# Per-head stationary blocks, K and Q turned and spread apart, and new orders on five engines

## The reference

```python
x = x + conv_block(group_norm(x))      # mask from centres of mass, relu, 3x3 conv, bias
x = x + ttt_block(group_norm(x))       # "test-time training" layer over the 784 tokens
```

```python
def step(carry, inp):                  # once per chunk, in order
    W1c, b1c = carry
    xq, xk, xv, et = inp
    Z1 = xk @ W1c + b1c
    grad = _ln_l2_bwd(Z1, xv - xk, g, bb)
    Attn1 = jnp.tril(xq @ xk.swapaxes(-1, -2))
    b1_bar = b1c - jnp.tril(et) @ grad
    Z1_bar = xq @ W1c - et * Attn1 @ grad + b1_bar
    last_eta = et[..., -1, :, None]
    W1n = W1c - (last_eta * xk).swapaxes(-1, -2) @ grad
    b1n = b1c - (last_eta * grad).sum(-2, keepdims=True)
    return ((W1n, b1n), xq + _ln(Z1_bar, g, bb, EPS_IN))
```

## Time and profile before

| | |
|---|---|
| median of 3 runs | 2133.62 us (2129.63 to 2134.75) |
| the profiled execution | 2131.73 us, its span 2129.9 us |
| PE busy, weight loads busy | 85%, 67% of the span |
| DVE, POOL, ACT busy | 73%, 63%, 55% |
| mean granted clock of TensorE | 0.632 of full speed |
| first and last start of a spread of K and Q | 474.1 and 2060.8 us |

### The profile page before, as it was taken

How to read it: one execution, slowest core, us unless ns; L and a number is a source line. 1 busy time by engine, 2 the same in 40 slices (tenths; PEclk the granted TensorE clock), 3 DMA queues, 4 the chain that set the end, 5 groups by cost and what they waited for, 6 DMA issues and landing times.

```text
span 2129.9 us, 81338 instructions
## 1 busy us (share of the span) xinstructions
PE 1804.8 (85%) x33518; PEld 1429.6 (67%) x33518; DVE 1553.4 (73%) x3818; ACT 1166.9 (55%) x2554; POOL 1336.7 (63%) x1479
## 2 busy tenths in 40 slices
PE   2868898715898988989989899998998989989887
PEld 1434454304777877778778787777777877778775
DVE  6989988416777777777777777777777777777764
ACT  2324545435556565566665556656566566565653
POOL 1253444474767776677766777667776777676763
PEclk9988999855556565555555555556555555555655
DMA  5085899843454545545455454464554545545444
GB/s 222 1 44 48 102 78 77 77 143 45 57 70 57 76 65 62 72 57 75 65 61 75 57 74 66 59 77 57 72 68 58 76 62 67 70 56 77 60 57 51
DMA packets 1148753, 148.76 MB, mean 70 GB/s; under 512 B 1128416, under 2 KB 1141984, under 8 KB 1148384
## 3 DMA queue, kind: packets, MB, share of 16 engines
q1 hardware_dynamic: 1148384, 143.57, 53.6%
HBM read 40.71 MB, written 38.54 MB: 37 GB/s over the span
## 4 chain that ended last, share of the span: by engine, by line
PE 59%; DVE 11%; ACT 8%; issue 6%; SPq 6%; DMA 6%; POOL 3%; ACTq 0%; POOLq 0%; DVEq 0%
PE p_kt L1604 11%; PE p_m L1617 8%; PE p_x L1632 7%; ACT work L820 7%; PE p_y L1674 6%; PE p_y L1632 6%; PE p_x L1656 5%; SPq L494 4%; PE p_j L1571 3%; PE p_j L1572 3%; DMA late<-work 3%; PE p_j L1573 2%; DMA xs_scratch<-work 2%; PE p_x L1623 2%; SPq L415 2%
## 5 line engine op out<-in xcount | busy, mean ns | idle before, releaser
L1604 PE MATMUL p_kt<-fold,kqk 128*128 128x16 f16 x6272 | 237.0, 180 | 143.9 <-ACT work L820 139.5
L1604 PEld LDWEIGHTS p_kt<-fold,kqk 128*128 128x128 f16 x6272 | 224.5, 117 | 183.1 <-issue 177.9
L820 ACT ACTIVATE work<-p_kt 128x256 f16<-128x256 f32 x392 | 256.6, 785 | 127.2 <-PE p_kt L1604 126.7
L1286 DVE TENSOR_TENSOR work<-work 128x256 f16<-128x256 f32 x196 | 147.8, 857 | 58.0 <-ACT work L801 58.0
L1632 PEld LDWEIGHTS p_x<-w,late 128*128 128x128 f16 x4704 | 178.1, 118 | 11.8
L1632 PEld LDWEIGHTS p_y<-w,late 128*128 128x128 f16 x4704 | 177.6, 118 | 11.1
L1656 PEld LDWEIGHTS p_x<-work,kqk 128*128 128x128 f16 x4704 | 172.2, 118 | 17.6 <-issue 13.2
L596 POOL TENSOR_TENSOR w<-wst,w 128x256 f16<-128x256 f32 x98 | 71.9, 734 | 175.2 <-ACT w L849 175.2
L1617 PE MATMUL p_m<-work,late 128*128 128x16 f16 x4704 | 164.4, 181 | 18.7 <-DVE lgt L1265 10.0
L1507 PE MATMUL p_j<-work 128*128 128x392 f16 x864 | 160.0, 347 | 22.4 <-DVE work L1101 20.7
L1617 PEld LDWEIGHTS p_m<-work,late 128*128 128x128 f16 x4704 | 160.8, 118 | 21.0 <-issue 10.8
(11 more groups left out here) (171 smaller groups left out, 4638.7 us busy)
## 6 DMA issues: line engine op xcount, KB each, us to landing
kqk<-work SPq DMA_DIRECT2D x392, 64.0 KB, 3.3
late<-work SPq DMA_DIRECT2D x392, 64.0 KB, 3.2
late<-work SPq DMA_DIRECT2D x392, 32.0 KB, 2.2
out_y<-work SPq DMA_DIRECT2D x49, 256.0 KB, 6.1
x_scratch<-late SPq DMA_DIRECT2D x24, 392.0 KB, 11.8
xs_scratch<-work SPq DMA_DIRECT2D x24, 392.0 KB, 6.3
work<-x_scratch SPq DMA_DIRECT2D x49, 192.0 KB, 3.2
work<-xs_scratch SPq DMA_DIRECT2D x48, 192.0 KB, 3.2
```

The lines of the kernel that those rows point to most:

```text
L820: last = act.activation(kqt16[:, o, g, :, :, :, :].rearrange("p q t e a -> p q (e a) t"), p_kt[:, o * SC:(o + 1) * SC].rearrange("p (q f t ...
L1286: last = dve.tensor_tensor(paired(hl16[:, c % 2, at, g:g + GP, :, :, :, 1]), in_pairs(qk[:, o, :]), paired(hl16[:, c % 2, at, g:g + GP, :, ...
L1604: mm = pe.matmul(p_kt[:, at:at + CS], part, fold16[:, :], start=True, stop=True)
```

## The change

Each head gets a block of its own in all three tiles, so that the columns of a stationary matrix step by 2 elements, 4 bytes, instead of 8. The run of bytes that a spread can copy at once becomes half as long (64 instead of 128 bytes), and there are twice as many. `fold_kq` becomes `fold_k` and `fold_q`: each turns K or Q of both groups of a half, still 32 matmuls and 512 columns of `p_kt`, and each is copied by one ACT instruction of 512 elements (`kt_copy`, `qt_copy`) in place of two of 256. The spread of the turned tile becomes two of 8 transfers each, `kt_spread` and `qt_spread`, both on SP. `z_state` and `k_dot_q` wait for the first, `outputs` for the second. `o_square` gets a tile `sqo` of its own in place of the one shared with `z_square`. Many steps get explicit waits for the reader before them. All five `turn(k)` have a new order.

```diff
-        mbd = second.cut([NG, NP, GB, CS, 2, 2], F16)
-        ktqt1 = second.cut([2, NG, NP, GB, CS, 2, 2], F16)
+        mbd = second.cut([NG, NH, GB, CS, 2], F16)
+        ktqt1 = second.cut([2, NG, NH, GB, CS, 2], F16)
...
-        kq_sets = [kqk[:, 0:2 * third].rearrange("p (s b e) -> p s b e", b=GB, e=4 * HD),
+        kq_sets = [kqk[:, 0:2 * third].rearrange("p (s b e) -> p s b e", b=GB, e=2 * HD),
...
+            def turned_spread(c, o, landed_sem):
+                part = kqt16[:, o, :, :, :, :].rearrange("p g h t a -> p (g h) (t a)")
+                whole = ktqt[c % 2][:, o, :, :, :, :, :].rearrange("p g h b t a -> p (g h) b (t a)")
+                for b in range(GB):
+                    at = slice(b * CS, (b + 1) * CS)
+                    sp.dma_start(whole[at, :, b, :], part[at]).then_inc(landed_sem, 16)
+
             @guard_chunk
             def kt_spread(c):
-                sp.wait_ge(kt_copy_done.sem, kt_copy_done.count("group1", 2 * c + 1))
+                sp.wait_ge(kt_copy_done.sem, kt_copy_done.count(2 * c + 1))
...
+                    sp.wait_ge(z_done.sem, z_done.count(2 * c - 3))
+                    sp.wait_ge(k_dot_q_done.sem, k_dot_q_done.count(c - 2))
+                turned_spread(c, 1, kt_landed.sem(c))
+
+            @guard_chunk
+            def qt_spread(c):
+                sp.wait_ge(qt_copy_done.sem, qt_copy_done.count(2 * c + 1))
...
+                turned_spread(c, 0, qt_landed.sem(c))
...
             def turn(k):
+                y_store(k - 6)
                 xs_next(k)
-                xr_load(k - 5)
-                kq_spread(k - 2)
-                y_store(k - 6)
                 m_spread(k - 3)
+                xr_load(k - 4)
                 kt_spread(k - 2)
+                qt_spread(k - 2)
+                kq_spread(k - 1)
...
+            def turned_copy(s, o):
+                g = GP * (s % 2)
+                return act.activation(kqt16[:, o, g:g + GP, :, :, :].rearrange("p g h t a -> p g a (h t)"),
+                                      p_kt[:, :].rearrange("p (g a n) -> p g a n", g=GP, a=2), ACT.Copy)
...
-                act.activation(paired(mc16[:, :, :, :, :, 0]), in_pairs(p_m[:, :]), ACT.Copy).then_inc(m_high_done.sem, 1)
+                act.activation(mc16[:, :, 0], p_m[:, :], ACT.Copy).then_inc(m_high_done.sem, 1)
...
             def kq_turned(c, o, g, h, a):
-                return ktqt[c % 2][:, o, g, h // 2, :, :, h % 2, a].rearrange("p b t -> p (b t)")
+                return ktqt[c % 2][:, o, g, h, :, :, a].rearrange("p b t -> p (b t)")
...
+            def fold(s, part_of):
+                c, g = s // 2, GP * (s % 2)
                 pe.wait_ge(kq_landed.sem(c), kq_landed.count(c))
...
+                for k in range(GP):
+                    for a in range(2):
+                        for h in range(NH):
+                            at = ((k * 2 + a) * NH + h) * CS
+                            mm = pe.matmul(p_kt[:, at:at + CS], part_of(g + k, h, a), fold16[:, :], start=True, stop=True)
+                return mm
...
             def z_hat(s):
+                if s >= 1:
+                    dve.wait_ge(g_dot_done.sem, g_dot_done.count(s - 1))
+                    dve.wait_ge(g_along_done.sem, g_along_done.count(s - 1))
```

More of the change, by code:

```diff
@@ L282, in program @@
         kt_landed = landed("kt_blocks", 2, GB)
+        qt_landed = landed("qt_blocks", 2, GB)
         m_landed = landed("m_blocks", 1, GB)
@@ L300, in program @@
         target_done = step("target")
-        fold_done = steps("fold", "group0 group1")
-        kt_copy_done = steps("kt_copy", "group0 group1")
+        fold_k_done = step("fold_k")
+        fold_q_done = step("fold_q")
+        kt_copy_done = step("kt_copy")
+        qt_copy_done = step("qt_copy")
         k_dot_q_done = step("k_dot_q")
@@ L524, in xr_load, with m_spread @@
                 sp.dma_start(xr[:, c % 2, FRONT:B, :], x2_t[:, :, CS * c:CS * (c + 1)].rearrange("b c n -> c b n")).then_inc(xr_landed.sem(c), 16)
+            @guard_chunk
+            def m_spread(c):
+                sp.wait_ge(m_low_done.sem, m_low_done.count(c))
+                sp.wait_ge(m_high_done.sem, m_high_done.count(c))
+                if c == 0:
+                    sp.wait_ge(s_m_zero, 1)
+                else:
+                    sp.wait_ge(o_done.sem, o_done.count(2 * c - 1))
+                part = mc16.rearrange("p (s t) a -> p s (t a)", t=CS)
+                whole = mbd.rearrange("p g h b t a -> p (g h) b (t a)")
+                for b in range(GB):
+                    at = slice(b * CS, (b + 1) * CS)
+                    sp.dma_start(whole[at, :, b, :], part[at]).then_inc(m_landed.sem(c), 16)
             def turn(k):
+                y_store(k - 6)
                 xs_next(k)
-                xr_load(k - 5)
-                kq_spread(k - 2)
-                y_store(k - 6)
                 m_spread(k - 3)
+                xr_load(k - 4)
                 kt_spread(k - 2)
+                qt_spread(k - 2)
+                kq_spread(k - 1)
             for k in range(NCH + 6):
@@ L800, in qk_high @@
                     at = o if c % 2 == 1 else 1 - o
-                    last = act.activation(paired(hl16[:, c % 2, at, g:g + GP, :, :, :, 0]), in_pairs(qk[:, o, :]), ACT.Copy)
+                    last = act.activation(hl16[:, c % 2, at, g:g + GP, :, 0], pair(qk[:, o, :]), ACT.Copy)
                 last.then_inc(qk_high_done.sem, 1)
@@ L1285, in qk_low @@
                     at = o if c % 2 == 1 else 1 - o
-                    last = dve.tensor_tensor(paired(hl16[:, c % 2, at, g:g + GP, :, :, :, 1]), in_pairs(qk[:, o, :]),
-                                             paired(hl16[:, c % 2, at, g:g + GP, :, :, :, 0]), ALU.subtract)
+                    last = dve.tensor_tensor(hl16[:, c % 2, at, g:g + GP, :, 1], pair(qk[:, o, :]),
+                                             hl16[:, c % 2, at, g:g + GP, :, 0], ALU.subtract)
                 last.then_inc(qk_low_done.sem, 1)
```

297 lines of the change are left out of this document (155 added, 142 removed).

## The result

| | before | after |
|---|---|---|
| median of the runs | 2132.75 us | 2112.1 us |
| lowest and highest | 2129.63, 2134.75 us | 2105.97, 2116.49 us |
| span of the profiled execution | 2129.9 us | 2111.3 us |

After is 0.9902 of before (95 % interval 0.9874 to 0.9931). It lies 50 us above the upper end of the range, 2062: the forecast was 178 us less, and 21 came.

The account below looks back on a forecast made before the run. PE's 30.2 us of work plus 2.7 waiting bound the 32.9 us turn; afterwards SP's issuing, 28.9 plus 0.3 for waits, makes 29.2. Over 48 turns, 2131.7 less 178 gives 1954 us, range 1880 to 2062.

Parts of the forecast that it names:

- Stationary step: PE weight loads at a 4-byte step: a pair falls from 33.4 to 26.7 ns, gaining 4.1 us a turn.
- Rival (5): PE weight loads: the step is free, pairs stay at 33.4 ns, turn 31.0 us, 2040 us; chance 0.07.
- Folds and copies: ACT's copy of a fold falls from 1.32 to 0.75 us; PE's wait for it from 2.7 to 0.3 us a turn.
- The sync queue takes over: SP's issuing becomes the bound: 23.2 us a turn plus 5.7 for eight Q issues, 28.9 us.
- The sum: Whole turn: the largest of the engines' times, SP's 28.9 us, plus 0.3 for waits, 29.2 us; total 1954 us.
- Does the queue stall in its new order?: SP between `kq_spread` and `kt_spread`: copies need 6.6 us of 10.6, so it fits with 3 us to spare.
- (3): DMA transfers bound: packets cost 16 ns or more, spreads land late, turn 31.5 us, 2064 us; chance 0.18.
- (4): Odd half's loop, `z_state` to `grad`: steps between need the old 17.9 us, turn 30.6, 2021 us; chance 0.09.
- (6): Odd half's loop needs more than the break-even 20.2 us; at 20.7, turn 33.4, slower at 2156 us; chance 0.05.
- (2): SP's issues nearer 0.635 us; DVE and POOL bound the turn at 26.5 to 28.2, about 1855 us; chance 0.11.

Follow-up runs that it names:

- orders and folds alone: The kernel after, with the old 8-byte pairs of two heads in all three tiles, keeping its new orders, split folds and 32 spread issues: 2013.5 us, ratio 0.9453.
- The step alone: The kernel before, with only the 4-byte layout of all three tiles; old orders, old folds, one turned spread of 8 transfers: 1988.0 us, ratio 0.9343.
- the two runs with 512: The kernel after, with 512-packet `kq_spread` transfers: half the packets left out, 2006.5 us; or all bytes sent, K-and-Q blocks in pairs, 2024.9 us.
- the run with the loads on ACT: The kernel after, with the output store and four loads of a turn issued from ACT's queue, nothing left out: 1920.5 us, ratio 0.9018.
- the run with seven transfers fewer: The kernel after, with only one of the eight `qt_spread` transfers made, the other turned Q blocks left zero: 1868.5 us, ratio 0.8773.

## Why the prediction was wrong

**Stationary step: right.** 26.7 ns a pair were forecast; 96 pairs in 2.71 us with a last matmul of 0.17 give 26.7. Rival (5), by the Trainium skill's rule (page SBUF — State Buffer, section on the DMA port swizzle) that 2-byte data may be strided up to 8 elements for free, is refuted for these weight loads: L1736's went from 118 to 104 ns at the median. In the run with the orders and folds alone, with the 8-byte step, they have 118 still. The step alone took 6.6 % off the kernel, its quicker copies included.

**Folds and copies: right.** A copy was forecast at 0.75 us and took 0.75, and PE's wait for it is gone. PE's own work came to 25.9 us, 26.1 forecast.

**The sync queue takes over: right as a mechanism, wrong in size.** This is the step that failed: "So 28.9 us." Measured are 32.5 us of issuing in the turn shown (32.3 on average over 38 turns), and 32.7 from turn to turn on average. The sum gave every old row its old price and the new issues nothing but theirs. Row by row against the earlier trace rows and the 5.7 us added for Q:

- the turned spreads 12.67 us, 11.4 forecast: +1.3. Most issues are still at 0.63 us, some at 1 to 2. Why those happen no run told.
- `kq_spread` 8.56 us, 6.96 forecast: +1.6. The prediction set this to nothing, with 1.3 as its other end: "is not cheaper, so no". `m_spread` and `kt_spread` of before had 256 and 512 packets, and between those two there is next to no difference (medians of 610 and 634 ns); the step comes at 1024, and from the third issue on, as the medians by place and the two runs with 512 showed.
- the load behind the store 3.02 us against 1.56: +1.5. Not foreseen at all. In the old order `m_spread` stood behind the store, and in the turn of the earlier trace rows it starts 1.85 us after the store's issue ends, so most of the stall passed in a wait. The new order puts a load right there and has hardly a wait left.
- `m_spread` 5.92 us against 6.95: −1.0. The store 0.84 against 0.62: +0.2. The gaps between the rows, 0.7 against the 0.3 added for waits.

The averages over 38 turns weigh this otherwise. By them the rows of before sum to 22.1 us; the 23.2 of the forecast came from one turn that happened to be 1.1 us longer, which hid as much of the error. From there the queue grew by 10.2 us, where 5.7 were forecast. The new orders added 6.0 for the turned spreads and 2.1 for the load behind the store (and took 0.4 from other rows); the doubled packets, on top of the new orders, added 1.2 to `kq_spread`, 0.6 to the turned spreads, 0.4 to `m_spread` and 0.3 to the rest. So the single row missed by most is the load behind the store, and the packets of all spreads together cost 2.5.

In the turn shown the differences sum to 4.0 us; over 48 turns the mean is 32.7 for 29.2, 3.5 us or 168 us in all, less the 10 us that the start and the emptying gave: the miss of 158.

That the old trace hid the stall in a wait is borne out by the step alone, which has the old order with little left to wait for. Its `m_spread` waits 6.6 us in 1400 (63.9 before), and its longest issue, 4 us, is a first of eight, directly behind the store:

```profile
SPq L508 <- DVE work L1300: 6.6, 10, 1.1
```

```profile
L508 SPq DMA_DIRECT2D late<-work x392: 586/632/3991, 509.0 to 1953.9; - x196
```

The median of those first issues is 3.4 us there, and 0.8 before.

**Does the queue stall in its new order? Right:** it hardly ever waits. For that reason every microsecond of issuing counts in full.

**Rivals.** (3), transfers bound, named nearly the measured turn (31.5) and its sign, PE waiting for `kqk` and `late` (6.6 us a turn). But the sync engine has no gaps, and the run with the loads on ACT moves the same packets in 28.8 us, so the engines' time for all packets is not the bound. Their share went from 53.6 to 56.0 % of the span only, for 1.44 times the packets. Yet (3) was not all wrong: the issues of a full queue grow with the packets ahead of them, and the one behind the store is held while all 16 engines are busy. Part of what is counted here as issuing is waiting for the queue's own transfers. What holds the sync engine in the other long issues is not shown. (4) and (6), the loop, are out by the run with seven transfers fewer. (2), cheaper issues, had the sign of the error the wrong way round.

**The range** ended at 2062, since I took the extremes of single rows and added none of them together; a queue without a gap adds all of them.

## What to carry to other kernels

When a change takes the bound to an issuing queue, cost every issue of that queue by the packets of the transfers that it stands behind, and look in the old trace for stalls that a wait hides; in a new order without waits they come due. Two changes that each pay (6.6 and 5.5 %) can pay nothing together when both draw on one queue. Moving issues to another engine's queue pays only for those that this engine can make where nobody waits for it, and only while the first queue bounds: five did (9.8 % under before), thirteen cost 3.6 %, and the same five cost 7 % once the turned spreads were one and the queue was no longer the bound.

## What was not expected of the hardware

- The time that the sync engine needs to issue a transfer was 609 ns at the median with 256 packets (L493 of the run with the old step, 32 KB), 632 with 512 packets of the same 32 KB (L535 of after), 635 with 512 packets of 64 KB, and 840 with 1024 packets of 64 KB. It goes by the packets of the transfers ahead: the first of eight issues with 1024 packets takes 0.60 us, and the store's issue, with 4096 of its own, 0.63 or 0.84 depending on what stands before it.

```profile
L493 SPq DMA_DIRECT2D late<-work x784: 585/609/1897, 483.6 to 1967.7; - x196
```

```profile
L535 SPq DMA_DIRECT2D late<-work x392: 586/632/3119, 513.6 to 2083.9; - x196
```

- The issue behind the store of 4096 packets takes 2.9 us, 1.9 behind 2048, at the median. With the store on another queue it takes 0.8, while two of the issues that meet the store go from 0.63 to 1.2 us.
- ACT began none of its own instructions behind three issues on its queue until they were made: 3.5 us for three, with both queues at work.
- In every kernel here some issues, at all places of the order, take 1 to 2 us instead of 0.63. What they meet stays open.
